# A q load moved ahead of the shifted V rows, with a third buffer, and half of a GELU moved ahead of a copy

## The reference, cut to what matters

```python
h = tok(x, ...)                                   # [64, 63, 128]
# attention on layernorm(h)
q = bn(x @ Wq + bq).reshape(b, H, DK, t)          # 8 heads of 16
k = softmax((x @ Wk + bk).reshape(b, 1, DK, t))
v = bn(x @ Wv + bv).reshape(b, 1, DK, t)
lam_c = einsum('bukt,buvt->bkv', k, v)
Yc = einsum('bhkt,bkv->bhvt', q, lam_c)
lam_p = relu(conv3x3(v, Wpos))
Yp = einsum('bhkt,bkvt->bhvt', q, lam_p)
h = h + (Yc + Yp).reshape(...).transpose(...) @ Wout + bout
# feed-forward on xf = layernorm(h)
y = experts(xf, top1(xf @ gate_w.T)) + gelu(xf @ sw1.T) @ sw2.T
h = h + y
```

## Time and profile before

| what | us |
|---|---|
| median of 3 executions | 703.7 |
| the three | 703.38, 703.7, 710.52 |
| the profiled execution | 709.8 |
| its span, first to last instruction | 708.0 |

### The profile page before, as it was taken

How to read it: one execution, slowest core, us unless ns; L and a number is a source line. 1 busy time by engine, 2 the same in 40 slices (tenths; PEclk the granted TensorE clock), 3 DMA queues, 4 the chain that set the end, 5 groups by cost and what they waited for, 6 DMA issues and landing times. The chain is left out here.

```text
span 708.0 us, 13451 instructions
## 1 busy us (share of the span) xinstructions
PE 609.9 (86%) x3740; PEld 488.0 (69%) x3740; DVE 501.3 (71%) x1381; ACT 279.2 (39%) x691; POOL 301.2 (43%) x303
## 2 busy tenths in 40 slices
PE   3789999999999999943799889888888619999995
PEld 1558888888888888822477677657666508888884
DVE  7878789999999887754447766667567235777774
ACT  4222333333333323113055564465464404555542
POOL 4733345555555333111134665665664621333333
PEclk9789999999999999975559997999999958999998
DMA  9003566655664555563222433332330111222220
GB/s 277 1 1 123 174 197 192 194 182 181 185 183 155 163 167 167 176 151 116 89 62 74 109 106 92 92 102 88 94 93 30 46 55 52 69 69 72 66 58 9
DMA packets 88227, 79.89 MB, mean 113 GB/s; under 512 B 27798, under 2 KB 81133, under 8 KB 87030
## 3 DMA queue, kind: packets, MB, share of 16 engines
q1 hardware_dynamic: 84886, 73.06, 34.9%
q0 software_dynamic: 3296, 6.27, 2.8%
HBM read 31.76 MB, written 48.09 MB: 113 GB/s over the span
## 5 line engine op out<-in xcount | busy, mean ns | idle before, releaser
L1015 DVE SCALAR_TENSOR_TENSOR P<-PS,QN 128x512 f32<-128x512 f32 x128 | 79.2, 681 | 57.9 <-PE PS L1134 57.9
L523 DVE SCALAR_TENSOR_TENSOR Z<-PS,Vt,Z 126x128 f32<-126x128 f32 x224 | 78.6, 351 | 8.4 <-PE PS L644 0.6
L644 PE MATMUL PS<-Wh,Ah 128*126 128x512 f32 x256 | 79.5, 434 | 0.0
L1281 POOL DMA_INDIRECT out_h<-OS,XS x39 | 37.9, 971 | 92.0 <-DVE OS L1325 91.6
L644 PE MATMUL PS<-Wl,Ah 128*126 128x512 f32 x256 | 72.7, 407 | 3.1 <-DVE Wl L487 3.1
L313 POOL TENSOR_TENSOR INCl<-INC,INCh 126x512 fp32r<-126x512 f32 x31 | 40.0, 1291 | 77.7 <-ACT INCh L390 77.7
L644 PE MATMUL PS<-Wh,Al 128*126 128x512 f32 x256 | 70.9, 399 | 0.0
L644 PEld LDWEIGHTS PS<-Wl,Ah 128*126 128x126 f32 x256 | 49.3, 193 | 15.9 <-issue 3.5
L644 PEld LDWEIGHTS PS<-Wh,Al 128*126 128x126 f32 x256 | 48.6, 190 | 12.7
L430 ACT ACTIVATE XT<-PS 128x126 f32<-128x126 f32 x32 | 8.9, 277 | 107.8 <-PE PS L690 107.8
L644 PEld LDWEIGHTS PS<-Wh,Ah 128*126 128x126 f32 x256 | 45.4, 194 | 8.3 <-issue 2.0
(11 more groups left out here) (224 smaller groups left out, 1612.3 us busy)
## 6 DMA issues: line engine op xcount, KB each, us to landing
routed<-nobody SPq DMA_DIRECT2D x30, 1170.0 KB, 5.2
IM<-v_pad SPq DMA_DIRECT2D x128, 78.8 KB
XS<-routed SPq DMA_DIRECT2D x39, 130.0 KB, 2.1
WRW<-in_w SPq DMA_DIRECT2D x16, 256.0 KB, 3.1
R<-h_rows SPq DMA_DIRECT2D x16, 129.9 KB
W1l<-in_wsig SPq DMA_DIRECT2D x4, 512.0 KB, 8.2
WR<-in_w SPq DMA_DIRECT2D x8, 256.0 KB, 7.8
q_raw<-QS SPq DMA_DIRECT2D x32, 63.0 KB
```

Source lines behind the costliest of these rows:

```text
L523: ins = dve.scalar_tensor_tensor(Z[:, u], psU[h][:, d], sc, Z[:, u], ALU.mult, ALU.add)
L644: ins = pe.matmul(out, a, w, start=(n == 0), stop=(n == len(turn) - 1))
L1015: ins = dve.scalar_tensor_tensor(P[:, b, HV * h:HV * h + HV], psC[2 * pair + hb], 0.0, QN[:, g % 2, b:b + 1].broadcast_to([128, HV, SP]), ...
L1281: pool.indirect_dma_start(out_rows, bass.IndirectOffsetOnAxis(XS[:, k % XB, IDC:IDC + 1].bitcast(i32), 0), OS[:, k % 2], None, bounds_chec ...
```

## The change

Three edits, all in `middle`. QR gets three buffers (`QB = 3`), with a semaphore each. On SyncE the q load of step k stands ahead of the eight loads of the shifted V rows and no longer waits for their condition; it waits for QN of the group that used its buffer before. On ScalarE the first half of the GELU of group g stands ahead of the copy LS. Two semaphores that were used once each (`pat_stored`, `pat_in`) become one (`pat`), which changes no order.

```diff
-        NM = NG // 2
+        NM, QB = NG // 2, 3
-        QR = sb("QR", [128, 2, GB, S])
+        QR = sb("QR", [128, QB, GB, S])
...
-                sp.dma_start(QR[:, g % 2], src).then_inc(q_in[g % 2], 16)
+                sp.dma_start(QR[:, g % QB], src).then_inc(q_in[g % QB], 16)
...
             for k in range(NG):
                 if on(k + 2, 0, NG):
+                    wait_from_one(sp, qn_ready, k)
+                    load_q(k + 2)
                     sp.wait_ge(conv_done, 4 * k + 4)
                     load_im(k + 2)
-                    sp.wait_ge(qn_ready, k + 1)
-                    load_q(k + 2)
...
-                    pool.wait_ge(q_in[w], 16 * ((k + 1) // 2 + 1))
+                    pool.wait_ge(q_in[(k + 1) % QB], 16 * ((k + 1) // QB + 1))
...
+                if on(g, 0, NG):
+                    gelu(g, 0)
                 if on(k + 1, 0, NG):
                     act.wait_ge(lam_done, k + 2)
                     wait_from_one(act, lc_ready, k + 1)
                     act.activation(LS[:], psL.rearrange("p b v -> p (b v)"), ACT.Copy).then_inc(ls_ready, 1)
-                if on(g, 0, NG):
-                    gelu(g, 0)
```

More of the change, by code:

```diff
@@ L761, in middle @@
         bn_ready, sdv_ready, bnp_ready, bnt_done, bnr_ready = sem("bn_ready"), sem("sdv_ready"), sem("bnp_ready"), sem("bnt_done"), sem("bnr_ready")
-        pat_stored, pat_in, w36_ready = sem("pat_stored"), sem("pat_in"), sem("w36_ready")
+        pat, w36_ready = sem("pat"), sem("w36_ready")
         ks_ready, exp_done, k_ready, v_ready, vn_ready = sem("ks_ready"), sem("exp_done"), sem("k_ready"), sem("v_ready"), sem("vn_ready")
         v_stored, kt_done, vt_done, kvt_ready = sem("v_stored"), sem("kt_done"), sem("vt_done"), sem("kvt_ready")
-        im_in, q_in = [sem("im_in0"), sem("im_in1")], [sem("q_in0"), sem("q_in1")]
+        im_in, q_in = [sem("im_in0"), sem("im_in1")], [sem(f"q_in{n}") for n in range(QB)]
         h_in, scattered = [sem(f"h_in{n}") for n in range(RB)], [sem(f"scattered{n}") for n in range(RB)]
@@ L822, in _ @@
             sp.wait_ge(bnr_ready, 1)
-            sp.dma_start(pat_q, BNR[0:2, :].unsqueeze(1).broadcast_to([2, S, F])).then_inc(pat_stored, 16)
-            sp.wait_ge(pat_stored, 16)
-            sp.dma_start(PQ[:], bass.AP(pat_q.tensor, 0, [[S, 128], [S * F, 2], [1, S]])).then_inc(pat_in, 16)
+            sp.dma_start(pat_q, BNR[0:2, :].unsqueeze(1).broadcast_to([2, S, F])).then_inc(pat, 16)
+            sp.wait_ge(pat, 16)
+            sp.dma_start(PQ[:], bass.AP(pat_q.tensor, 0, [[S, 128], [S * F, 2], [1, S]])).then_inc(pat, 16)
             sp.wait_ge(v_ready, 2)
@@ L853, in _ @@
             L.link(pool.memset(QN[:, :, :, S:SP], 0.0))
-            pool.wait_ge(pat_in, 16)
+            pool.wait_ge(pat, 32)
             def scatter(g):
@@ L877, in step @@
                 if on(k + 1, 0, NG):
-                    pool.wait_ge(q_in[w], 16 * ((k + 1) // 2 + 1))
+                    pool.wait_ge(q_in[(k + 1) % QB], 16 * ((k + 1) // QB + 1))
                     wait_from_one(pool, p_ready, 4 * k)
                     wait_from_one(pool, yc_done, k)
-                    L.link(pool.tensor_tensor(QN[:, w, :, 0:S], QR[:, w], PQ[:, 0:1].broadcast_to([128, GB, S]), ALU.mult))
+                    L.link(pool.tensor_tensor(QN[:, w, :, 0:S], QR[:, (k + 1) % QB], PQ[:, 0:1].broadcast_to([128, GB, S]), ALU.mult))
                     pool.tensor_tensor(QN[:, w, :, 0:S], QN[:, w, :, 0:S], PQ[:, 1:2].broadcast_to([128, GB, S]), ALU.add).then_inc(qn_ready, 1)
```

## The result

The changed kernel took 684.2 us (median of 4 executions, 681.78 to 687.68), the kernel before 707.1 beside it on the same chip (median of 4, 703.38 to 712.56). The ratio is 0.970, with a 95% interval of 0.964 to 0.976: about 21 us less. The forecast was 688.5, or 0.978 of 703.7.

What follows compares the result with a forecast made beforehand. TensorE's waits were taken as the loss: 12.4 us before `down` for Gl, 7.8 before `up` for X2l. Steps 3 to 14 go from 160.07 to 145.9; with 1.0 for step 15 the gain is 15.2, 703.7 to 688.5 us, range 682 to 698.

Steps and rivals of the forecast that it cites:

- The rebuilt steps: Steps 3 to 14 of `middle` recomputed: late ones 12.04 odd and 10.92 even, steps 5 to 10 12.84 and 11.72 us.
- Part 1: Earlier q load on SyncE: X2l no longer stands late behind QN, saving `up`'s idle time, 7.8 us over 9 places.
- Part 2: First GELU half ahead of LS on ScalarE: `down` starts 1.0 us earlier, only 0.2 in steps 5 to 10.
- the 1.0 of step 15: Step 15's gain from the moved GELU half, 1.0 us, added to the gain of steps 3 to 14.
- I leave these 3.35 us in: Extra time of steps 6 and 7, where the clock was down, kept in the forecast: 142.56 becomes 145.9 us.
- Part 2 hidden: Rival: something unseen holds `down`, so the GELU move's gain is lost: 695.9 us; chance 0.07.
- VectorE held by QN: Rival: QN delays VectorE's norm of the rows, 0.8 us uncovered in 13 places: 698.9 us; chance 0.05.
- the clock rival: Fewer TensorE waits keep the clock up in steps 6 and 7, 3.35 us more gained: 685.2 us; chance 0.15.
- The higher group: Rival: the changed kernel's median falls among slower executions, one of three being 6.8 us over the median: 695; chance 0.10.
- q late: Rival: q still lands after 10.4 us, so the q load's gain is lost: 696.3 us; chance 0.05.
- nothing: Rival: another engine takes over both waits, so neither edit does anything: 703 us; chance 0.04.
- the slower case: Rival: IM lands after its conv behind the q load, TensorE stands still each step: 711.3 us; chance 0.04.

Runs made afterwards that it cites:

- q part alone: Changed kernel with the first GELU half back behind the copy LS; q load ahead of IM and three q buffers kept: 697.1 us, ratio 0.983.
- the scatter behind LC: Changed kernel with GpSimd's two scatters moved from the end of its step to behind LC of the next, h load one group later: 681.8 us, 0.961.
- filler in front: Kernel before with only the GELU half moved, plus eight matmuls on constants before `up`'s wait for X2l: 700.7 us, 0.986.
- the additions on GpSimd: Changed kernel with two additions into an unread tile on GpSimd between XTg and X2l, making X2l late: 746.4 us, 1.052.

## Why the prediction was right, and where it was off

**What bounds the kernel.** Right. The two waits of TensorE named from the earlier trace rows are where the time came from, with the clock behind them, and the experiments reach each of them.

**The rebuilt steps.** The mechanism was right, and its sizes nearly so. Late steps of the changed kernel take 11.7 and 10.7 us (12.04 and 10.92 forecast), early ones 12.65 and 11.6 (12.84 and 11.72). Part 1: the kernel with the q part alone has 149.26 us for steps 3 to 14; against 160.07 less the 3.35 of the clock this is a gain of 7.5, forecast 7.8. Part 2 on top of it: from 149.26 to 141.12 or 140.46, 8.1 to 8.8, forecast 6.4 (7.4 with the 1.0 of step 15). By the steps, it is 1.2 in late ones and 0.3 in early ones, where I had taken 1.0 and 0.2. So between my two bounds for `down`, 0.89 by TensorE's row and 1.3 by Gl's, the truth was nearer the second.

**The step that failed** is "I leave these 3.35 us in". The clock had been a rival with a chance of 0.15, as something that fewer waits might or might not do. It is a part of the mechanism. The five profiles in which `up` waits for X2l for 7.8 us or more, from 350 us to the end of the steps, have low steps (2 and 5 for the kernel before, then 8, 7 and 12). The others have none: the wait is 0.2 us in most, 2.2 with the scatter behind LC, and 4.8 with filler in front. The filler shows that the cause is TensorE standing idle, and not X2l's lateness as such; the additions on GpSimd show it from the other side. The 3.35 also came from a profile with little of it: the second profile of the kernel before has five low steps and 165.60 us. Taking 160.07 and 165.60 against 141.12 and 140.46 gives 19 to 25 us, which holds the 21 of the medians; the forecast's sum, 15.2, was low by this term above all. Without the clock the sum holds: from 156.7 (160.07 less 3.35) to 141.12 or 140.46 is 15.6 to 16.3 us in steps 3 to 14, where 14.2 were forecast. The Trainium skill, "TensorE: Matmul & The Clock Gate", section "What's actually happening", has activity as what releases the throttle; both experiments agree.

**"About half of it from each part"** is right only for Part 2 on top of Part 1. By itself Part 2 gains nothing (1.005), Part 1 by itself about 12 us, both 21. The working held the reason without drawing it: X2l stands behind QN, QN behind q, and so as long as q is late the time at which `up` starts is set by SyncE's queue, whatever the GELU does. The rival "Part 2 hidden" had Part 1 working and Part 2 lost; what the runs show is that Part 2 is lost when Part 1 is missing.

**The queue.** "The q that is late here isn't needed until the next step" was right, and so was the distance: issued 4.98 us into step 12 instead of the 6.03 taken, and used at 492.63, 9.1 us later (8.1 forecast). What the prediction took over unchanged was the time to land. In the second profile of the changed kernel the q load has:

```profile
DMA to landing us min/median/max: 2.4/4.7/10.6
```

The median was 7.7 before and is 3.8 with the q part alone, so ahead of IM most loads also land sooner. The longest, 10.6, is beyond the 8.3 taken as the worst, yet QN has no wait for q in the list. IM's wait didn't come: from 350 to 570 us no wait for IM has a row among the waits.

**VectorE held by QN** came, and was hidden. The norm beside QN, timelines of VectorE and GpSimd in step 10:

```profile
459.17 1.25 DVE L1066 TENSOR_SCALAR R<-R,MV,SD 126x128 f32<-126x128 f32 x2
```

```profile
458.85 0.68 POOL L881 TENSOR_TENSOR QN<-QR,PQ 128x252 f32<-128x252 f32 x1
459.61 0.73 POOL L882 TENSOR_TENSOR QN<-QN,PQ 128x252 f32<-128x252 f32 x1
```

The pair ends at 460.42, right behind QN at 460.34. That QN holds the norm up agrees with the Trainium skill, "SBUF — State Buffer", section "Who interferes with whom", as cited in the prediction. That it waits for the whole of QN isn't shown: a norm begun only behind QN would have ended its own 0.34 us later, not 0.08. Over the kernel, by instructions of the line:

```profile
L1066 DVE TENSOR_SCALAR R<-R,MV,SD x32: 334/347/879, 353.4 to 526.9; 126x128 f32<-126x128 f32 x32
```

Before, the longest of the 32 was 0.349 (0.750 in the second profile). The total is 13.4 us, 2.4 above 32 times the median of before (0.344). TensorE didn't wait for it. Its transposes of the normed rows in step 10 start here, 0.96 us after the norm has ended, with no idle time in front:

```profile
461.38 0.39 PE L1213 MATMUL PS<-K,R 126*128 126x126 f32 x2
```

In steps 4 to 14 of both profiles this distance is 0.57 us or more. In return the 1.00 us of the earlier trace rows is gone: that line's longest is now 0.194.

**The range and the other rivals.** 684.2 lies in 682 to 698, near its lower end and beside the 685.2 of the clock rival. The higher group, q late, nothing, and the slower case didn't come.

## What to carry to other kernels

An engine's idle time is cheap or dear by what stands behind it in its queue. Here 45 us of GpSimd's waiting, with X2l behind it, cost TensorE 8 us of waiting and low clock besides; the same 45 us cost next to nothing once GpSimd waited for TensorE's own output. When a transfer is late, try its place in the issuing queue before another buffer: here the place was the whole gain. Two waits in one chain don't add: remove first the one that would swallow the other's gain. And if TensorE's short waits come with a granted clock below 1.00, expect them to cost more than their length.

## What the runs showed of the hardware

- 128 useless matmuls made a kernel some 10 to 13 us faster; the granted clock of twelve steps went from 0.89 to 1.00 and their time from 164.93 to 155.50 us.
- 14.5 us of delay spread over twelve steps, 1.21 in each, lengthened them by 53 us, at a clock of 0.75. No idle stretch of TensorE in them was longer than 1.37 us.
- In steps 1 and 2 TensorE has no gaps (busy 28.52 of 28.53 us) and yet the clock is at 1.2 GHz for most of them; in two of the profiled executions it came back earlier (23.7 and 23.8 us, at 0.79 and 0.80). What decides this, nothing here shows.
